# Seven unread copies beside each 8-column product of a two-layer recurrence

## What is computed

```python
pre = jnp.einsum('bsi,hi->bsh', inp, W_ih) + (b_ih + b_hh)
def step(h, p_t):
    h = jnp.tanh(p_t + h @ W_hh.T)
    return (h, h)
_, hs = jax.lax.scan(step, h0, jnp.swapaxes(pre, 0, 1))
```

## Time and profile before

| | us |
|---|---|
| median of 3 runs | 1154.31 (1153.18 to 1155.77) |
| span of the profiled execution | 1152.6 |
| the median above that span | 1.7 |
| PE busy | 1094.6 (95%) |
| PE weight loads busy | 935.8 (81%) |
| ACT busy | 787.2 (68%) |
| DVE busy | 699.3 (61%) |
| POOL busy | 144.5 (13%) |

### The profile page before, as it was taken

How to read it: one execution, slowest core, us unless ns; L and a number is a source line. 1 busy time by engine, 2 the same in 40 slices (tenths; PEclk the granted TensorE clock), 3 DMA queues, 4 the chain that set the end, 5 groups by cost and what they waited for, 6 DMA issues and landing times.

```text
span 1152.6 us, 62476 instructions
## 1 busy us (share of the span) xinstructions
PE 1094.6 (95%) x26880; PEld 935.8 (81%) x26880; DVE 699.3 (61%) x3140; ACT 787.2 (68%) x4577; POOL 144.5 (13%) x220
## 2 busy tenths in 40 slices
PE   4799999999999999999999999999899879889998
PEld 2699999999999999999999999999744368823333
DVE  7565455555555555555555544444456769899996
ACT  1466777777777777777777777677567878666664
POOL 4200000000000000000000000000003302331210
PEclk9555555555555555555555555555599989999999
DMA  4000000000000000000000000000000000256686
GB/s 143 8 9 10 9 9 14 9 9 9 10 13 10 9 9 9 10 14 9 9 5 5 4 5 5 5 4 5 3 1 1 1 1 1 86 212 228 247 285 204
DMA packets 30594, 47.22 MB, mean 41 GB/s; under 512 B 12322, under 2 KB 21611, under 8 KB 30316
## 3 DMA queue, kind: packets, MB, share of 16 engines
q1 hardware_dynamic: 29772, 43.08, 11.2%
q10 hardware_dynamic: 544, 0.13, 0.0%
HBM read 40.84 MB, written 2.36 MB: 37 GB/s over the span
## 4 chain that ended last, share of the span: by engine, by line
PE 86%; DVE 5%; ACT 3%; POOL 2%; issue 2%; DMA 1%; SPq 1%; DVEq 0%; POOLq 0%; ACTq 0%
PE bank L656 44%; PE bank L752 7%; PE bank L1403 6%; PE bank L735 5%; PE bank L1708 5%; PE bank L426 4%; PE bank L525 3%; PE bank L730 2%; PE bank L1436 1%; PE bank L747 1%; PE bank L1585 1%; PE bank L411 1%; PE bank L446 1%; PE bank L315 1%; PE bank L1493 1%
## 5 line engine op out<-in xcount | busy, mean ns | idle before, releaser
L656 PE MATMUL bank<-space,whh_hi 128*128 128x8 f16 x16384 | 609.5, 169 | 7.4 <-DVE space L783 4.4
L656 PEld LDWEIGHTS bank<-space,whh_hi 128*128 128x128 f16 x16384 | 528.4, 105 | 25.3 <-DVE space L783 7.4
L783 DVE TENSOR_TENSOR space<-h_f,space 128x16 f16<-128x16 f32 x2048 | 291.5, 176 | 380.4 <-ACT h_f L764 378.8
L764 ACT ACTIVATE h_f<-bank 128x16 f32<-128x16 f32 x2048 | 300.1, 184 | 229.8 <-PE bank L656 222.4
L770 ACT ACTIVATE space<-bank 128x16 f16<-128x16 f32 x2048 | 299.0, 184 | 1.1 <-PE bank L656 1.1
L656 PE MATMUL bank<-space,whh_lo 128*128 128x32 f16 (+1 forms) x2096 | 145.0, 190 | 0.0
L752 PE MATMUL bank<-space,wih_hi 128*128 128x32 f16 x2048 | 137.1, 188 | 0.0
L426 PE MATMUL bank<-onehot,tab 128*128 128x128 f16 x448 | 116.7, 266 | 0.5 <-DVE prepare_cur L476 0.5
L735 PE MATMUL bank<-xr,wih_hi 128*128 128x32 f16 x512 | 109.8, 214 | 0.0
L730 PE MATMUL bank<-ones,bias 128*128 128x32 bf16 x512 | 102.9, 201 | 0.0
L656 PEld LDWEIGHTS bank<-space,whh_lo 128*128 128x128 f16 x2096 | 102.2, 107 | 0.0
(11 more groups left out here) (303 smaller groups left out, 1637.8 us busy)
## 6 DMA issues: line engine op xcount, KB each, us to landing
space<-weights_kept SPq DMA_DIRECT2D x64, 512.0 KB, 7.7
space<-in_x SPq DMA_DIRECT2D x28, 129.0 KB, 3.1
out<-res SPq DMA_DIRECT2D x7, 256.0 KB, 9.9
space<-in_wrec SPq DMA_DIRECT2D x1, 768.0 KB, 4.1
space<-in_wx SPq DMA_DIRECT2D x1, 740.5 KB, 9.0
brec<-in_brec SPq DMA_DIRECT2D x1, 260.0 KB
ew<-in_ew SPq DMA_DIRECT2D x1, 256.0 KB, 4.1
weights_kept<-wturned SPq DMA_DIRECT2D x8, 32.0 KB, 1.8
```

What stands on the lines that cost most here:

```text
L656: mm = pe.matmul(own[:, m, :], w[:, k, m * P:(m + 1) * P], steps(h, k), start=False, stop=False, skip_group_check=True)
L764: act.activation(h_f[layer][:, s % 2, :, :], own, ACT.Tanh, scale=scale[layer]).then_inc(s_h[layer], 1)
L783: dve.tensor_tensor(h[layer][:, :, s % RINGS[layer], 1, :], h_f[layer][:, s % 2, :, :], h[layer][:, :, s % RINGS[layer], 0, :], ALU.subtra ...
```

## The change

`low` and `high` no longer call `add` but a new `add_wide`. Its products have the same weights and the same waits and signals. The moving operand is the same 8 columns of the state, repeated eight times through a broadcast dimension of step 0 (64 columns streamed), and the result goes to eight places of the bank: `wide_sums(layer, s)` takes the whole bank of 512 columns as (j, m, s, b) and gives (m, j, b) for one step. Copy j = 0 is the place that `sums` gives; j = 1 to 7 lie in columns 64 to 511, are accumulated like the first and are read by nothing. `rest_of_high` keeps `add`.

```diff
+COPIES = 8
...
+        def wide_sums(layer, s):
+
+            own = bank[layer * 3 + s // U % 3].rearrange("p (j m s b) -> p m s j b", m=KH, s=U, b=B)
+            return own[:, :, s % U, 0:COPIES, :]
...
+        def add_wide(pe, own, w, state):
+
+            for m in range(KH):
+                for k in range(KH):
+                    mm = pe.matmul(own[:, m, :, :], w[:, k, m * P:(m + 1) * P],
+                                   state[:, k, :].unsqueeze(1).to_broadcast([P, COPIES, B]),
+                                   start=False, stop=False, skip_group_check=True)
+            return mm
...
             def low(layer, s):
                 if 0 <= s < T:
                     pe.wait_ge(s_lo[layer], OPEN + s)
                     at = (s - 1) % RINGS[layer]
-                    add(pe, sums(layer, s // U)[:, :, s % U, :], whh_hi[layer], h[layer],
-                        lambda h, k: h[:, k, at, 1, :]).then_inc(s_sum[layer], 1)
+                    add_wide(pe, wide_sums(layer, s), whh_hi[layer],
+                             h[layer][:, :, at, 1, :]).then_inc(s_sum[layer], 1)
...
             def high(layer, s):
...
-                    add(pe, sums(layer, s // U)[:, :, s % U, :], whh_hi[layer], h[layer],
-                        lambda h, k: h[:, k, at, 0, :]).then_inc(s_part[layer], 1)
+                    add_wide(pe, wide_sums(layer, s), whh_hi[layer],
+                             h[layer][:, :, at, 0, :]).then_inc(s_part[layer], 1)
```

## The result

The changed kernel takes **1174.6 us** (median of 4 runs, 1172.6 to 1175.4) against 1154.6 for the kernel before, measured beside it: a ratio of 1.0169, 95% interval 1.0155 to 1.0184. It is slower by 20 us, where 15.8 were forecast (1170, range 1147 to 1186).

What follows compares the result with a forecast made beforehand. The prediction took a 0.753 us latency chain per slot, not PE's work, as the bound. From a span of 1152.6, +15.0 + 2.3 - 1.5 gave 1168.4; with runs 1.7 above the span, the forecast was 1170 us, range 1147 to 1186.

Steps and rivals of the forecast that it cites:

- The loop as the bound, and what the width does to it: Recurrence slot: a latency chain of low products, tanh and difference sets its length; wide products lengthen it by 0.025 us.
- The floor: Shortest slot set by the chain of latencies in the recurrence: 0.753 us before, claimed 0.778, bounds 0.753 to 0.853.
- The clock: TensorE in the recurrence: granted clock rises a few us after both layers run, from about 50 us, and stays up.
- The rival in which it stays at 1.2 GHz: Recurrence: PE becomes the bound at 1.12 us a slot, about 1519 us; chance 0.08 including a clock falling now and then.
- PE's queue at the full clock: PE's work per recurrence slot: 0.66 to 0.78 us, under the loop; excess falls from 0.011 to 0.001, bounds 0 and 0.004.
- The steady part: All 1,024 recurrence slots: mean slot from 0.7643 to 0.779 us, +15.0 us in all, bounds -11.6 to +91.
- Before the clock rises: First slots at 1.2 GHz: five lengthen by about 0.11 us, the next four to six grow to 1.12; +2.3 us (0.5 to 5).
- After the last slot: Output and first feed-forward products after the recurrence: half the time if the clock is still up; -1.5 us (0 to -2.8).
- That the floor doesn't rise: Rival, recurrence slot: the awaited end comes no later, only PE's excess goes, 1143.5 us; chance 0.10.
- the estimate from the two formulas of the Trainium skill: Low products: 189 ns for 8 columns, 192.5 for 64, so a floor 3.5 ns higher, about 1147.5 us in all.
- The repeated pattern: Rival, wide products: the repeated operand streams at half speed, slots of 0.88 us or more, at least 1273 us; chance 0.03.
- visible idle time of PE: Sign that the forecast is right: in the recurrence PE shows idle time that ends on L783, the difference.

## Why the prediction was right, and where not

**The loop as the bound, and what the width does to it** held. The floor was put at 0.753 rising to 0.778, by 0.025; the shortest slots went from 0.754 to 0.775. The last low product took 0.193, as the row of L446 had it. The rise is a little smaller because the three starts before it were taken as unchanged: the first two are 39 ns apart in place of 48, the next two gaps 29 in place of 27 (medians where PE is not late), which with the 25 of the last product makes 0.021.

**The clock** was forecast up after both layers run, about 50 us, and to stay. It rose at 46.3, while layer 1 had not yet begun its low products, and stayed to 845.0. The rival in which it stays at 1.2 GHz fell with that. With two copies PE is busy for 700.00 of 700.00 us and the granted clock is 0.50. That a TensorE kept busy gets the full clock, the rule of the Trainium skill, "TensorE: Matmul & The Clock Gate", in "Why this matters for your kernels", that the prediction weighed, is contradicted by this trace once more.

**PE's queue at the full clock** is the step that was sized wrong. The excess over the floor was to fall from 0.011 to 0.001, at most 0.004, and is 0.005 to 0.006. I priced the seven other products at 27 ns or less and the 128-column ones at 0.06, and left out L525, whose products are 62 to 71 ns apart at either clock; with weight loads of 0.096 in place of 0.14 to 0.17 its slots are long no more. The trace of the kernel before had it: 130 of its 143 slots above 0.79 hold L525. The steady part came out at (0.7809 - 0.7643) x 1,024 = +17.0 for +15.0, the rise of the floor being a little smaller and the excess larger than forecast.

**Before the clock rises**, +2.3 was given; it is +0.8. There are eight slots of 0.89 in the mean, a little over 0.10 longer than later ones and some 0.13 longer than the loop before, where 0.11 was given. One lies between these rows of the changed kernel:

```profile
41.91 0.61 PE L670 MATMUL bank<-space,whh_hi 128*128 128x64 f16 x8
42.79 0.61 PE L670 MATMUL bank<-space,whh_hi 128*128 128x64 f16 x8
```

The slots of 1.12, with both layers at the lower clock, never came.

**After the last slot**, -1.5 was given and +2.7 came. The last of the 1,024 slots starts at 839.66 (821.97 before), so of the 20.4 us between the spans, 1173.0 and 1152.6, 17.7 lie up to there and 2.7 behind. The clock was down from 845.0 to 855.2, so the output products and first feed-forward products ran at the lower clock as before, and the thin slots ahead of them, with wide products at the lower clock, lost 0.7. It was down again for a few us from 903 and from 1022.6, each time with PE busy; set against the same products of the kernel before, counted from the last slot, those behind the first fall come 1.5 later and those behind the second another 1.4. Some of this is won back between. Two further falls, at 947 and at 1039.5, left no lasting loss; the kernel before has one, from 924.9 to 935.1. A full clock in the recurrence is not needed for such falls: the kernel with two copies, whose recurrence runs at 0.50 like that of the kernel before, has one at the place of the second.

```profile
1006.90:1010.10 3.20, 3.20 (x18) 1.77 (x15) 2.25 (x4) 1.26 (x3) 0.74 (x1) 0.50 0.92 301
```

Behind the last low product nothing was changed, but in the kernel with other weights for L531; the time from there to the end still differed by 3.0 us between the kernels' profiles, 322.1 to 325.1. What decides where the clock falls there was not tried and stays open. The three terms were off by 2.0 (steady part), -1.5 (before the rise) and 4.2 (after the last slot); that two of them partly cancel is luck, and so is in part the size of the third.

**The rivals.** That the floor doesn't rise fell by the 0.33 to the tanh. With it fell the estimate from the two formulas of the Trainium skill, same page, "Single matmul latency" (a floor higher by 3.5 ns gives 1147.1 by the prediction's own sum, not 1147.5): for the lower clock they give 189 ns for 8 columns, where the trace of the kernel before has 168; 16 columns took 174 in the kernel with two copies. The repeated pattern costs nothing: wide products start 29 ns apart, as those of L1413 without repetition do. What was said of visible idle time of PE was wrong: within 80 to 800 us it shows none, since the modelled ends of its products cover the wait.

## What to carry to other kernels

When small dependent products sit in a loop with other engines, find the one product whose end is awaited, and price a change by what it does to that end; the rest of PE's work is free until its queue is longer than the loop. Columns added to raise the clock belong on products that nobody waits for at once: the same added columns made this kernel 1.4% slower on the awaited products and 1.5% faster on the others. The number of copies has a best value between a clock that falls back and a queue that grows.

## What was not expected of the hardware

Weights read at every sixteenth element load in 140 to 173 ns, neighbouring ones in 95 to 98 at the full clock (mostly 104 to 107 at half), and the former doesn't change with the clock. A narrow product right behind wide ones took 170 ns and its reader started 39 ns after its end, where 166 and 36 were usual. With four copies in the high products alone the clock went up and down some forty times in one execution, and it lost only 0.8% against the kernel with six (0.9871 against 0.9795), as its loop is nearly as long at either clock (0.742 and 0.754).
